# Two-layer graph network on one core: bias matmul, softmax division and loops of the stage between the layers, rewritten

## Chip, cores and metric

One NeuronCore of a Trainium2 chip. The metric is the device time of one execution in microseconds (us).

## What is computed

A graph of N = 6250 nodes with 128 features and E = 106250 edges sorted by destination. The reference, cut to what matters:

```python
h = relu(layernorm(x))
# layer 0: softmax over the edges of each node, feature by feature, then a linear layer
msg   = h[src] + edge_attr
e     = exp(msg*beta - segment_max(msg*beta)[dst])
denom = segment_sum(e, dst)                      # [N, 128]
agg   = segment_sum(msg * e / denom[dst], dst)   # [N, 128]
x     = x + (agg @ H + bias + h)                 # H: 128x128 from phm_rule and W
# layer 1: graph attention, 4 heads
h  = relu(layernorm(x))
Wx = h @ W.T                                     # [N, 128], then edge scores, softmax, sum, elu
x  = x + elu(attention(Wx, a, src, dst))
```

The bias is a row of 128 float32 numbers, drawn at random, so it is not zero.

## The kernel before

**Edges.** Edges go in 208 groups of 512. In both layers GpSimd issues indirect DMAs for the rows of the source nodes, TensorE turns tiles and sums edges into nodes by one-hot matmuls, VectorE scans for the running maximum, and ScalarE takes exponentials and adds each group's sums to `acc`, in which the nodes lie along the free axis: `acc[:, 0, n]` is the numerator of node n and `acc[:, 1, n]` its denominator, with the 128 features on the partitions. The last group of layer 0 is merged by `L659`.

**Between the layers.** 6250 nodes are 49 tiles of 128, in 13 batches (`NBAT`) of 4 tiles (`GE` = 512 nodes), of which the last has one tile of 106 nodes. For each batch:

- `invert0` (VectorE, `L958`): reciprocal of the 512 denominators of each partition into `inv`, one of two buffers that lie in `ring_h`.
- `average0` (GpSimd, `L577`): numerator times reciprocal into `aggT`, one of two buffers, also in `ring_h`. From the third batch on it waits for `mid_out` of two batches before.
- `layer_out` (TensorE): for each of the 4 tiles, a float32 matmul of `aggT` with the matrix `phm` (`L1156`), and a float32 matmul that adds the bias, with a row of ones as its weights, one partition deep (`L1158`). It writes one of two PSUM banks of `sums`.
- `finish0` (VectorE): adds the result to `nodes` (`L966`), and takes statistics of the 4 tiles for the layer norm (`statistics`, `L768`).

When all 13 batches are measured, `norm_all_nodes` makes the scale and shift of every node (22 small VectorE instructions, `L777` to `L790`). Then GpSimd copies those of a batch to `norm_b` (`numbers1`, `L530`), ScalarE makes relu of the normalised tiles (`h1`, `L699`), TensorE turns them (`L1169`) and multiplies by W (`L1181`), VectorE copies out, and SyncE stores the rows that layer 1 gathers.

**Order.** Each engine has a loop written by hand, `sweep(eng, count, unroll, stages)`: step s calls every stage for item s - lag, in the order listed. VectorE has `[(3, finish0), (0, invert0)]`, GpSimd `[(1, average0)]`, TensorE `[(2, layer_out)]`. The first and last steps are written out and those between are a hardware loop (`Fori`). Engines wait for one another by semaphores alone.

Of the kernel before, what the change touches and what calls it, by code (L numbers as in the profile page):

```python
# [56 lines left out]


def gnn_kernel(nc, x_in, src_in, dst_in, ea_in, rule_in, w0_in, bias_in, beta_in, w1_in, a_in, out):
    N, D = x_in.shape
# [13 lines left out]
    LAST = N - (NT - 1) * P  # L78
    NBAT = -(-NT // GB)
# [11 lines left out]
    HRING = 4  # L91
# [3 lines left out]
    with ctx:  # L95
        def sb(name, shape, dt=F32):
            return ctx.enter_context(nc.sbuf_tensor(name, shape, dt))

        def sem(name):
            return ctx.enter_context(nc.semaphore(name))  # L100

        def sems(name, n):
            return [sem(f"{name}{i}") for i in range(n)]
# [8 lines left out]
        ident = sb("ident", [P, P])  # L112
# [7 lines left out]
        ones_row = sb("ones_row", [1, P])  # L120
        junk = sb("junk", [1, 1])
        zero_row = sb("zero_row", [1, WIN], BF16)
        beta = sb("beta", [P, 1])
        bias_row = sb("bias_row", [1, D])
# [20 lines left out]
        nodes = sb("nodes", [P, NT, D])  # L145
        hn = sb("hn", [P, 2, GB, D])
# [10 lines left out]
        inv = ring_h[:, 0:2, :]  # L157
# [12 lines left out]
        acc = sb("acc", [P, 2, N + WIN])  # L170
# [13 lines left out]
        prod = sb("prod", [P, 2, GB, D])  # L184
        onehot = sb("onehot", [P, RING, GB, P])
        onehotT = sb("onehotT", [P, 2, GE])
        logit_v = sb("logit_v", [P, GB * H])
        logit = sb("logit", [P, WGT, GB * H])
        logit_d = sb("logit_d", [P, 2, GB * H])
# [5 lines left out]
        sums = ctx.enter_context(nc.psum_tensor("sums", [P, 2, 2, WIN], F32))  # L195
# [4 lines left out]
        bank = [ctx.enter_context(nc.psum_tensor(f"bank{i}", [P, GE], F32)) for i in range(4)]  # L200
# [31 lines left out]
        normed = sem("normed")  # L232
# [2 lines left out]
        ln0_part = sem("ln0_part")  # L235
        ln0_sum = sems("ln0_sum", WXB)
        h_stored = sems("h_stored", WXB)
        mid_inv = sem("mid_inv")
        mid_agg = sem("mid_agg")
        mid_out = sem("mid_out")  # L240
        mid_numbers = sem("mid_numbers")
        mid_h = sem("mid_h")
        mid_hT_psum = sem("mid_hT_psum")
        mid_hT = sem("mid_hT")
# [44 lines left out]
        L0, L1 = layer_sems(0), layer_sems(1)  # L289
# [20 lines left out]
        def _(sp):  # L310
# [176 lines left out]
        def _(pool):  # L487
# [32 lines left out]
            pool.memset(ones_row[:, :], 1.0).then_inc(self_pool, 1)  # L520
# [41 lines left out]

            sweep_edges(pool, [(0, gather0)])

            def numbers1(b, u, use):
                if later(b, 2):
                    pool.wait_ge(mid_h, b - 1)
                batch_numbers(b, u, mid_numbers)


            def average0(b, u, use):
                w = LAST if isinstance(b, int) and b == NBAT - 1 else GE
                pool.wait_ge(mid_inv, b + 1)
                if later(b, 2):
                    pool.wait_ge(mid_out, b - 1)
                apart(pool)
                pool.tensor_tensor(aggT[:, u, 0:w], acc[:, 0, bass.ds(b * GE, w)], inv[:, u, 0:w], ALU.mult  # L577
                                   ).then_inc(mid_agg, 1)
# [32 lines left out]
        def _(act):  # L611
# [78 lines left out]
            sweep_edges(act, [(5, merge0), (0, lift0), (3, weigh0)])  # L690


            def h1(b, u, use):
                act.wait_ge(mid_numbers, b + 1)
                if later(b, 2):
                    act.wait_ge(mid_hT_psum, b - 1)
                apart(act)
                for t in range(1 if isinstance(b, int) and b == NBAT - 1 else GB):
                    ins = act.activation(hn[:, u, t, :], nodes[:, bass.ds(b * GB + t, 1), :].rearrange("p a d -> p (a d)"),  # L699
                                         ACT.Relu, bias=norm_b[:, u, 1, t:t + 1], scale=norm_b[:, u, 0, t:t + 1])  # L700
                ins.then_inc(mid_h, 1)

            sweep(act, NBAT, 2, [(0, h1)])

            def weigh1(g, s, use):
                act.wait_ge(L1["shifted"], g + 1)
# [45 lines left out]
        def _(dve):  # L752
# [201 lines left out]
            def invert0(b, u, use):  # L954
                w = LAST if isinstance(b, int) and b == NBAT - 1 else GE
                if later(b, 2):
                    dve.wait_ge(mid_agg, b - 1)
                dve.reciprocal(inv[:, u, 0:w], acc[:, 1, bass.ds(b * GE, w)]).then_inc(mid_inv, 1)  # L958

            def finish0(b, u, use):  # L960
                last = isinstance(b, int) and b == NBAT - 1
# [3 lines left out]
                tiles = nodes[0:rows, b * GB:b * GB + 1, :] if last else nodes[:, bass.ds(b * GB, GB), :]  # L965
                dve.tensor_tensor(tiles, tiles, sums[0:rows, u, 0, 0:t * D].rearrange("p (t d) -> p t d", d=D), ALU.add  # L966
                                  ).then_inc(self_res, 1)
# [109 lines left out]
        def _(pe):  # L1077
# [68 lines left out]
            def layer_out(b, u, use):
                last = isinstance(b, int) and b == NBAT - 1
                pe.wait_ge(mid_agg, b + 1)
                if later(b, 2):
# [3 lines left out]
                for t in range(1 if last else GB):  # L1153
                    rows = LAST if last else P
                    where = sums[0:rows, u, 0, t * D:(t + 1) * D]
                    pe.matmul(where, aggT[:, u, t * P:t * P + rows], phm[:, :, :].rearrange("p j b -> p (j b)"),  # L1156
                              start=True, stop=False, skip_group_check=True)
                    ins = pe.matmul(where, ones_row[0:1, 0:rows], bias_row[0:1, :], start=False, stop=True,  # L1158
                                    skip_group_check=True)
                ins.then_inc(mid_out, 1)  # L1160

            sweep(pe, NBAT, 2, [(2, layer_out)])

            def turn_h(b, u, use):
                pe.wait_ge(mid_h, b + 1)
# [103 lines left out]
```

## Time and profile before

| | |
|---|---|
| time, median of 3 runs | 2384.46 us (2381.5 to 2385.74) |
| time of the profiled execution | 2380.09 us |
| its span | 2378.3 us |
| TensorE busy | 1833.2 us, 77% |
| VectorE busy | 2133.7 us, 90% |
| ScalarE busy | 1335.0 us, 56% |
| GpSimd busy | 1647.5 us, 69% |
| TensorE's mean granted clock, 1 is 2.4 GHz | 0.935 |

The profiled execution took 1.79 us more than its span, which goes from the first instruction to the last. Busy shares are means over four unlike stages: start, layer 0, the stage between the layers, and layer 1. Everything of the change lies in the third, which is some 3% of the span, so the rows below are those of that stage, with some from elsewhere that show what an instruction of a kind takes.

### The profile page before, as it was taken

Reading aid. Unit: us, or ns where it says so; the run is one execution under the profiler, and the core shown is the slowest. Engines: PE = TensorE matmul, PEld = TensorE weight load, DVE = VectorE, ACT = ScalarE, POOL = GpSimd, SP = SyncE. Lnnn points to the kernel's source line nnn. Section 1 sums busy time; section 2 is a strip of 40 time slices with the busy share of each in tenths; the row PEclk is TensorE's granted clock in tenths of the full one; section 3 lists DMA queues with packets and bytes.
Section 4 is the critical chain, followed back from the end, with each engine's and each line's share of the span. In section 5 each row is a group of like instructions: output and inputs, shape, how many; then the busy total and the mean of one; then the engine's idle time right before and its main releaser. Section 6 shows DMA issues by size and latency. Waiting matters only on the chain.

```text
span 2378.3 us, 61655 instructions
## 1 busy us (share of the span) xinstructions
PE 1833.2 (77%) x14239; PEld 1681.1 (71%) x14240; DVE 2133.7 (90%) x4065; ACT 1335.0 (56%) x3451; POOL 1647.5 (69%) x1748
## 2 busy tenths in 40 slices
PE   0466666666666766666787989999999998999986
PEld 0466666666666666666566888888888888888886
DVE  5799999999999999999766888888888888898885
ACT  2366666666666666666223555555555555555554
POOL 3677777777777777777115777777777777777761
PEclk9999999999999999999757999999999999999985
DMA  5544444444444444443003333333333333333321
GB/s 126 143 131 129 131 129 130 131 127 124 130 127 132 129 130 131 129 130 108 3 15 87 61 59 60 59 58 59 59 59 58 58 59 59 59 59 58 59 52 54
DMA packets 338740, 214.13 MB, mean 90 GB/s; under 512 B 170817, under 2 KB 305197, under 8 KB 338686
## 3 DMA queue, kind: packets, MB, share of 16 engines
q0 software_dynamic: 53248, 112.57, 20.0%
q1 hardware_dynamic: 285438, 100.94, 16.6%
q8 instruction: 22, 0.36, 0.1%
q14 instruction: 32, 0.26, 0.0%
HBM read 201.32 MB, written 10.30 MB: 89 GB/s over the span
## 4 chain that ended last, share of the span: by engine, by line
POOL 44%; issue 20%; DVE 18%; PE 6%; DMA 6%; SPq 3%; ACT 2%; DVEq 1%; POOLq 1%; ACTq 0%
POOL msg L590 24%; POOL ring_h L559 20%; DVE seg_max L900 5%; DVE run_max L897 3%; DMA ring_h<-h_dram,meta_g 3%; DMA msg<-wx_dram,meta_g 3%; DVE sums L897 2%; DVE prod L935 2%; DVE msg L918 2%; PE sums L1156 1%; PE sums L1158 1%; SPq L457 1%; PE sums L1115 1%; DVE onehot L944 1%; DVE onehot L881 1%
## 5 line engine op out<-in xcount | busy, mean ns | idle before, releaser
L559 POOL DMA_INDIRECT ring_h<-h_dram,meta_g x832 | 809.6, 973 | 259.9 <-issue 258.4
L590 POOL DMA_INDIRECT msg<-wx_dram,meta_g x832 | 792.6, 953 | 264.6 <-issue 246.0
L1115 PE MATMUL sums<-onehot,prod 128*128 128x128 f32 x3328 | 697.3, 293 | 25.0 <-ACT acc L659 12.8
L1115 PE MATMUL sums<-onehot,wgt 128*128 128x128 f32 x3328 | 678.5, 288 | 0.0
L1115 PEld LDWEIGHTS sums<-onehot,prod 128*128 128x128 f32 x3328 | 538.5, 204 | 71.0 <-issue 68.1
L1115 PEld LDWEIGHTS sums<-onehot,wgt 128*128 128x128 f32 x3328 | 540.2, 204 | 0.0
L1124 PE MATMUL bank<-beta_ident,msg 128*128 128x128 f32 x1664 | 245.7, 292 | 341.9 <-DVE msg L918 341.8
L1124 PEld LDWEIGHTS bank<-beta_ident,msg 128*128 128x128 f32 x1664 | 205.5, 195 | 382.5 <-DVE msg L918 331.2
L659 ACT ACTIVATE acc<-sums 128x1022 f32 x414 | 423.7, 1023 | 0.0
L688 ACT ACTIVATE sums<-ring_h 128x512 f32<-128x512 f32 x208 | 125.1, 602 | 382.1 <-DMA ring_h<-h_dram,meta_g 381.9
L897 DVE TENSOR_TENSOR_SCAN sums<-flags,seg_max,bank 4x512 f32<-4x512 bf16 x207 | 264.0, 1275 | 5.8 <-PE bank L1211 4.4
L897 DVE TENSOR_TENSOR_SCAN run_max<-flags,run_max,bank 128x512 f32<-128x512 bf16 x207 | 263.5, 1273 | 0.0
L900 DVE TENSOR_TENSOR_SCAN seg_max<-flags,run_max 128x512 f32<-128x512 bf16 x208 | 254.6, 1224 | 7.1
L900 DVE TENSOR_TENSOR_SCAN seg_max<-flags,sums 4x512 f32<-4x512 bf16 x208 | 251.1, 1207 | 7.2
L651 ACT ACTIVATE carried<-acc,scale 128x2 f32 x414 | 120.9, 292 | 184.5 <-PE sums L1115 175.7
L1202 PEld LDWEIGHTS bank<-window,onehotT 128*128 128x128 f32 x1664 | 212.1, 200 | 4.1 <-ACT onehotT L721 2.9
L1202 PE MATMUL bank<-window,onehotT 128*128 128x4 f32 x1664 | 206.0, 247 | 2.8 <-DMA window<-wx_dram 1.3
L709 ACT ACTIVATE sums<-logit_d 128x16 f32<-128x16 f32 x208 | 39.0, 188 | 267.8 <-DVE logit_d L1022 266.0
L881 DVE TENSOR_SCALAR onehot<-iota_f,meta_g 128x128 f32<-128x128 f32 x832 | 180.4, 275 | 6.0 <-DMA meta_g<-meta 5.9
L918 DVE TENSOR_TENSOR msg<-msg,sums 128x512 f32<-128x512 f32 x208 | 141.0, 678 | 13.2 <-ACT sums L688 13.1
L1030 DVE TENSOR_TENSOR prod<-sums,msg 128x512 f32<-128x512 f32 x208 | 140.0, 673 | 4.8 <-PE sums L1115 4.5
L935 DVE TENSOR_TENSOR prod<-sums,msg 128x512 f32<-128x512 f32 x208 | 142.0, 683 | 1.8 <-ACT sums L676 1.8
(144 smaller groups left out, 2750.5 us busy)
## 6 DMA issues: line engine op xcount, KB each, us to landing
msg<-in_edge_attr SPq DMA_DIRECT2D x207, 256.0 KB, 3.1
flags<-flag_dram SPq DMA_DIRECT2D x52, 512.2 KB
ring_h<-h_dram,meta_g POOLq DMA_INDIRECT x832
msg<-wx_dram,meta_g POOLq DMA_INDIRECT x832
window<-wx_dram SPq DMA_DIRECT2D x832, 2.0 KB
wx_dram<-msg SPq DMA_DIRECT2D x13, 272.0 KB, 2.5
nodes<-in_x SPq DMA_DIRECT2D x4, 768.0 KB, 8.3
h_dram<-wgt SPq DMA_DIRECT2D x12, 256.0 KB, 2.4
```

Source lines behind the costliest of these rows:

```text
L559: pool.indirect_dma_start(hg[:, s % HRING, b, :], None, h_dram, bass.IndirectOffsetOnAxis(ap=meta_g[:, s, b:b + 1], axis=0)).then_inc(L0[" ...
L590: pool.indirect_dma_start(msg[:, s, b, :], None, wx_dram, bass.IndirectOffsetOnAxis(ap=meta_g[:, s, b:b + 1], axis=0)).then_inc(L1["gather ...
L659: act.activation(acc[:, :, bass.ds(node + 1, WIN - 1)], sums[:, par, :, 1:WIN], ACT.Copy).then_inc(k["merged"], 1)
L881: ins = dve.tensor_scalar(onehot[:, s, b, :], iota_f[:, :], key[:, b:b + 1], None, ALU.is_equal)
L897: dve.tensor_tensor_scan(run, flag[:, 0:GE], data, before, ALU.add, ALU.max).then_inc(k["scanned"], 1)
L900: dve.tensor_tensor_scan(seg_max[0:n, par, ::-1], flag[:, GE:0:-1], run[:, ::-1], -BIG, ALU.add, ALU.max).then_inc(k["scanned"], 1)
L918: dve.tensor_tensor(msg[:, s, :, 0:D], msg[:, s, :, 0:D], row_psum.rearrange("p (b d) -> p b d", b=GB), ALU.add).then_inc(L0["added"], 1)
L935: dve.tensor_tensor(prod[:, s % 2, :, :], wgt_psum.rearrange("p (b d) -> p b d", b=GB), msg[:, s, :, 0:D], ALU.mult).then_inc(L0["multipli ...
L1030: dve.tensor_tensor(prod[:, s % 2, :, :].rearrange("p b (h d) -> p b h d", h=H), head, msg[:, s, :, 0:D].rearrange("p b (h d) -> p b h d", ...
L1115: ins = pe.matmul(sums[:, 0, j, bass.ds(off, P)], what[:, slot, b, :], onehot[:, s, b, :], start=(b == 0), stop=(b == GB - 1), skip_group_ ...
L1124: ins = pe.matmul(bank[s % 2][:, b * P:(b + 1) * P], msg[:, s, b, 0:D], beta_ident[:, :], start=True, stop=True)
L1202: ins = pe.matmul(bank[2][:, b * H:(b + 1) * H], onehotT[:, s % 2, b * P:(b + 1) * P], window[:, s, b, :], start=True, stop=True)
```

## The change

**Bias.** The bias row is loaded onto all 128 partitions (`bias_all`), and VectorE splits it into three bfloat16 parts, high, middle and low, whose sum is the float32 number. A tile `bias_parts` has the three parts in its first three partitions and zero in the others, repeated for the 4 tiles of a batch. One bfloat16 matmul of all 128 partitions against ones (`ones_parts`), 512 columns wide, puts the bias under a batch before the four `phm` matmuls add to it. The splitting is nine VectorE instructions after the layer 0 loop and ahead of its wait for the last merge.

**Division.** ScalarE takes `Ln` of the denominators and then `Exp` with scale -1 twice, once into a PSUM bank and once into `ring_h`: both are a first guess r of 1/d (`seed0`). GpSimd multiplies d by r (`polish0`). VectorE makes (d r - 2) r in PSUM and then multiplies that by -1 and by the numerator (`divide0`), which is one Newton step and the division. `ring_h` and the banks are rings of four, `diff` of two.

**Loops.** `sweep` gives way to `straight`, which writes all 13 batches out. VectorE's order is now `divide0` of batch s, then `finish0` of batch s - 2. `h1` reads the scale and shift from `norm` itself, so GpSimd's copies to `norm_b` for layer 1 go.

```diff
+def straight(count, stages):
+    for s in range(count + max(lag for lag, _ in stages)):
+        for lag, stage in stages:
+            if 0 <= s - lag < count:
+                stage(s - lag)
...
-            sp.dma_start(bias_row[:, :], bias_in.rearrange("(a d) -> a d", a=1)).then_inc(weights_in, 16)
+            sp.dma_start(bias_all[:, :], bias_in.rearrange("(a d) -> a d", a=1).to_broadcast([P, D])).then_inc(weights_in, 16)
...
-            sweep(pool, NBAT, 2, [(1, average0)])
-            pool.wait_ge(normed, 2)
-            sweep(pool, NBAT, 2, [(0, numbers1)])
+            def polish0(b):
+                w = LAST if b == NBAT - 1 else GE
+                pool.wait_ge(mid_seed, b + 1)
+                if b >= 2:
+                    pool.wait_ge(mid_inv, b - 1)
+                pool.tensor_tensor(diff[:, b % 2, 0:w], acc[:, 1, b * GE:b * GE + w], ring_h[:, b % HRING, 0:w], ALU.mult
+                                   ).then_inc(mid_near, 1)
+            straight(NBAT, [(0, polish0)])
...
+            act.wait_ge(L0["merged"], NG)
+            def seed0(b):
+                w = LAST if b == NBAT - 1 else GE
+                if b >= HRING:
+                    act.wait_ge(mid_out, b - HRING + 1)
+                near = ring_h[:, b % HRING, 0:w]
+                act.activation(near, acc[:, 1, b * GE:b * GE + w], ACT.Ln).then_inc(mid_log, 1)
+                act.wait_ge(mid_log, b + 1)
+                act.activation(bank[b % HRING][:, 0:w], near, ACT.Exp, scale=-1.0)
+                act.activation(near, near, ACT.Exp, scale=-1.0).then_inc(mid_seed, 1)
+            straight(NBAT, [(0, seed0)])
+            act.wait_ge(normed, 2)
...
+            part_of_bias(dve.tensor_copy(bias_hi, bias_all[:, :]))
+            part_of_bias(dve.tensor_tensor(bias_rest, bias_all[:, :], bias_hi, ALU.subtract))
...
-                dve.reciprocal(inv[:, u, 0:w], acc[:, 1, bass.ds(b * GE, w)]).then_inc(mid_inv, 1)
+            def divide0(b):
+                w = LAST if b == NBAT - 1 else GE
+                near = bank[b % HRING][:, 0:w]
+                dve.wait_ge(mid_near, b + 1)
+                dve.scalar_tensor_tensor(near, diff[:, b % 2, 0:w], 2.0, near, ALU.subtract, ALU.mult).then_inc(mid_inv, 1)
+                dve.wait_ge(mid_inv, b + 1)
+                dve.scalar_tensor_tensor(ring_h[:, b % HRING, 0:w], near, -1.0, acc[:, 0, b * GE:b * GE + w],
+                                         ALU.mult, ALU.mult).then_inc(mid_agg, 1)
...
-            sweep(dve, NBAT, 2, [(3, finish0), (0, invert0)])
+            straight(NBAT, [(0, divide0), (2, finish0)])
...
+            def layer_out(b):
+                last = b == NBAT - 1
+                t, rows = (1, LAST) if last else (GB, P)
+                if b >= 2:
+                    pe.wait_ge(self_res, b - 1)
+                elif b == 0:
+                    pe.wait_ge(L0["merged"], NG)
+                pe.matmul(sums[0:rows, b % 2, 0, 0:t * D], ones_parts[:, 0:rows],
+                          bias_parts[:, 0:t, :].rearrange("p t d -> p (t d)"), start=True, stop=False, skip_group_check=True)
+                pe.wait_ge(mid_agg, b + 1)
+                for i in range(t):
+                    ins = pe.matmul(sums[0:rows, b % 2, 0, i * D:(i + 1) * D],
+                                    ring_h[:, b % HRING, i * P:i * P + rows], phm[:, :, :].rearrange("p j b -> p (j b)"),
+                                    start=False, stop=(i == t - 1), skip_group_check=True)
+                ins.then_inc(mid_out, 1)
+            straight(NBAT, [(0, layer_out)])
```

## Rows read from the trace of the kernel before

**Rows 1.** Stretches of the middle stage, and one in layer 1 (windows: busy us and count).
```profile
core 0: us, PE busy (x) PEld busy (x) DVE busy (x) ACT busy (x) POOL busy (x), PEclk, DMA share, GB/s
...
1153.05:1157.90 4.85, 0.00 (x0) 0.00 (x0) 4.85 (x2) 0.00 (x0) 1.28 (x1) 0.76 0.00 0
1157.90:1229.70 71.80, 70.85 (x196) 48.80 (x196) 55.05 (x74) 0.00 (x0) 14.48 (x12) 0.50 0.00 0
1229.70:1235.27 5.57, 0.00 (x0) 0.00 (x0) 4.42 (x22) 0.00 (x0) 0.28 (x2) 0.50 0.00 0
...
1288.00:1295.40 7.40, 6.90 (x35) 6.54 (x36) 6.93 (x18) 1.98 (x5) 5.57 (x7) 0.50 0.34 62
```

**Rows 2.** Groups by line and shape, 1140 to 1260 us (busy us, mean ns, idle before).
```profile
L1156 PE MATMUL sums<-phm,ring_h 128*128 128x128 f32 x96 | 38.2, 501 | 6.8 <-POOL ring_h L577 6.8
L1158 PE MATMUL sums<-bias_row,ones_row 1*128 1x128 f32 x96 | 38.1, 498 | 0.0
...
L958 DVE RECIPROCAL ring_h<-acc 128x512 f32<-128x512 f32 x6 | 19.8, 3324 | 6.4 <-ACT acc L659 6.4
L699 ACT ACTIVATE hn<-nodes,norm_b 128x128 f32 x40 | 15.7, 480 | 0.3 <-PE bank L1169 0.3
L577 POOL TENSOR_TENSOR ring_h<-acc,ring_h 128x512 f32<-128x512 f32 x12 | 15.4, 1280 | 71.3 <-PE sums L1158 43.4 <-DVE ring_h L958 27.9
```

**Rows 3.** Waits, 1153 to 1229.7 us (total us, times, longest).
```profile
POOL ring_h L577 <- PE sums L1158: 47.9, 11, 4.6
```

**Rows 4.** Timeline of VectorE in the middle stage (start us, us).
```profile
1181.31 0.69 DVE L966 TENSOR_TENSOR nodes<-nodes,sums 128x512 f32 x1 [1.01 <-PE sums L1158]
...
1187.08 0.69 DVE L966 TENSOR_TENSOR nodes<-nodes,sums 128x512 f32 x1 [0.56 <-PE sums L1158]
...
1215.88 0.69 DVE L966 TENSOR_TENSOR nodes<-nodes,sums 128x512 f32<-128x512 f32 x1 [0.52 <-PE sums L1158]
1216.67 0.87 DVE L768 BATCH_NORM_STATS2 stats<-nodes 128x6 f32<-128x128 f32 x4
1217.46 0.80 DVE L958 RECIPROCAL ring_h<-acc 128x106 f32<-128x106 f32 x1
```

**Rows 5.** Timeline of ScalarE near the end of the kernel.
```profile
2340.97 0.63 ACT L735 ACTIVATE elu_e<-ring_h 128x512 f32<-128x512 f32 x1 [2.98 <-DVE ring_h L1049]
2341.63 0.63 ACT L737 ACTIVATE elu_e<-elu_e 128x512 f32<-128x512 f32 x1
2342.17 0.61 ACT L745 ACTIVATE hn<-acc 128x512 f32<-128x512 f32 x1
```

**Rows 6.** Timeline of GpSimd and TensorE in the stage.
```profile
1156.56 1.28 POOL L577 TENSOR_TENSOR ring_h<-acc,ring_h 128x512 f32<-128x512 f32 x1 [25.95 <-DVE ring_h L958]
...
1157.94 0.76 PE L1156 MATMUL sums<-phm,ring_h 128*128 128x128 f32 x2 [6.82 <-POOL ring_h L577]
...
1187.13 1.28 POOL L577 TENSOR_TENSOR ring_h<-acc,ring_h 128x512 f32<-128x512 f32 x1 [4.50 <-PE sums L1158]
```

**Rows 7.** Timeline of VectorE in layer 0, two independent instructions.
```profile
1083.51 0.68 DVE L918 TENSOR_TENSOR msg<-msg,sums 128x512 f32<-128x512 f32 x1
...
1084.11 0.69 DVE L944 TENSOR_TENSOR onehot<-bank,meta_g 128x512 f32<-128x512 f32 x1
```

**Rows 8.** Timeline of TensorE in layer 1, inside the last stretch of rows 1.
```profile
1292.57 0.63 PE L1115 MATMUL sums<-onehot,prod 128*128 128x128 f32 x2
1292.99 0.63 PE L1115 MATMUL sums<-onehot,wgt 128*128 128x128 f32 x2
```

**Rows 9.** Timeline of ScalarE at its first instructions.
```profile
30.80 1.28 ACT L630 ACT_TABLE_LOAD   x1 [30.67 <-PE bank L1086]
...
32.09 0.28 ACT L630 ACTIVATE meta<-bank 128x128 int32<-128x128 f32 x1
```

**Rows 10.** Groups by line and shape, whole span, VectorE: two SCALAR_TENSOR_TENSOR groups.
```profile
L1063 DVE SCALAR_TENSOR_TENSOR pos<-ring_h,nodes 128x512 f32<-128x512 f32 x12 | 8.2, 682 | 0.2 <-DVE ring_h L1049 0.2
...
L845 DVE SCALAR_TENSOR_TENSOR nodes<-run_max,nodes 128x512 f32 x4 | 3.8, 954 | 0.0
```

More of the change, by code:

```diff
@@ L119, in gnn_kernel @@
         head_pick = sb("head_pick", [P, H])
-        ones_row = sb("ones_row", [1, P])
         junk = sb("junk", [1, 1])
@@ L123, in gnn_kernel @@
         beta = sb("beta", [P, 1])
-        bias_row = sb("bias_row", [1, D])
+        bias_all = sb("bias_all", [P, D])
+        bias_parts = sb("bias_parts", [P, GB, D], BF16)
+        ones_parts = sb("ones_parts", [P, P], BF16)
         rule_rep = sb("rule_rep", [P, PH, PH])
@@ L156, in gnn_kernel @@
         hg = ring_h[:, :, :].rearrange("p r (b d) -> p r b d", d=D)
-        inv = ring_h[:, 0:2, :]
         inv_head = sb("inv_head", [P, GB * H])
@@ L186, in gnn_kernel @@
         onehotT = sb("onehotT", [P, 2, GE])
+        bias_hi, bias_mid, bias_lo = (hn[:, 0, i, :].bitcast(BF16)[:, 0:D] for i in range(3))
+        bias_rest = hn[:, 1, 0, :]
         logit_v = sb("logit_v", [P, GB * H])
@@ L237, in gnn_kernel @@
         h_stored = sems("h_stored", WXB)
+        bias_step = sem("bias_step")
+        bias_made = sem("bias_made")
+        mid_log = sem("mid_log")
+        mid_seed = sem("mid_seed")
+        mid_near = sem("mid_near")
         mid_inv = sem("mid_inv")
@@ L240, in gnn_kernel @@
         mid_out = sem("mid_out")
-        mid_numbers = sem("mid_numbers")
         mid_h = sem("mid_h")
@@ L519, in _ @@
             pool.tensor_copy(iota_f[:, :], iota_i[:, :]).then_inc(self_pool, 1)
-            pool.memset(ones_row[:, :], 1.0).then_inc(self_pool, 1)
+            pool.memset(ones_parts[:, :], 1.0).then_inc(self_pool, 1)
             pool.memset(zero_row[:, :], 0.0).then_inc(self_pool, 1)
@@ L563, in _ @@
             sweep_edges(pool, [(0, gather0)])
[L565 to L578, printed above, removed]
-            sweep(pool, NBAT, 2, [(1, average0)])
-            pool.wait_ge(normed, 2)
-            sweep(pool, NBAT, 2, [(0, numbers1)])
+            def polish0(b):
[6 more added lines that the diff above has]
+            straight(NBAT, [(0, polish0)])
             def gather1(g, s, use):
@@ L690, in _, with h1 @@
             sweep_edges(act, [(5, merge0), (0, lift0), (3, weigh0)])
-            def h1(b, u, use):
-                act.wait_ge(mid_numbers, b + 1)
-                if later(b, 2):
+            act.wait_ge(L0["merged"], NG)
[10 more added lines that the diff above has]
+            act.wait_ge(normed, 2)
+            def h1(b):
+                if b >= 2:
                     act.wait_ge(mid_hT_psum, b - 1)
[L697 to L700, printed above, removed]
+                for t in range(1 if b == NBAT - 1 else GB):
+                    n = b * GB + t
+                    ins = act.activation(hn[:, b % 2, t, :], nodes[:, n, :], ACT.Relu,
+                                         bias=norm[:, 1, n:n + 1], scale=norm[:, 0, n:n + 1])
                 ins.then_inc(mid_h, 1)
-            sweep(act, NBAT, 2, [(0, h1)])
+            straight(NBAT, [(0, h1)])
             def weigh1(g, s, use):
@@ L949, in _, with part_of_bias, finish0 @@
             sweep_edges(dve, [(0, add0), (0, one_hot0), (3, products0), (1, maxima0)])
-            dve.wait_ge(L0["merged"], NG)
[L954 to L957, printed above, removed]
-                dve.reciprocal(inv[:, u, 0:w], acc[:, 1, bass.ds(b * GE, w)]).then_inc(mid_inv, 1)
-            def finish0(b, u, use):
-                last = isinstance(b, int) and b == NBAT - 1
+            parts = [0]
+            def part_of_bias(ins):
+                parts[0] += 1
+                ins.then_inc(bias_step, 1)
+                dve.wait_ge(bias_step, parts[0])
+            part_of_bias(dve.tensor_copy(bias_hi, bias_all[:, :]))
+            part_of_bias(dve.tensor_tensor(bias_rest, bias_all[:, :], bias_hi, ALU.subtract))
+            part_of_bias(dve.tensor_copy(bias_mid, bias_rest))
+            part_of_bias(dve.tensor_tensor(bias_rest, bias_rest, bias_mid, ALU.subtract))
+            part_of_bias(dve.tensor_copy(bias_lo, bias_rest))
+            part_of_bias(dve.tensor_scalar(bias_rest, bias_hi, ident[:, 0:1], None, ALU.mult))
+            part_of_bias(dve.scalar_tensor_tensor(bias_rest, bias_mid, ident[:, 1:2], bias_rest, ALU.mult, ALU.add))
+            part_of_bias(dve.scalar_tensor_tensor(bias_rest, bias_lo, ident[:, 2:3], bias_rest, ALU.mult, ALU.add))
+            dve.tensor_copy(bias_parts[:, :, :], bias_rest.rearrange("p (a d) -> p a d", a=1).to_broadcast([P, GB, D])
+                            ).then_inc(bias_made, 1)
+            dve.wait_ge(L0["merged"], NG)
+            def divide0(b):
[6 more added lines that the diff above has]
+                                         ALU.mult, ALU.mult).then_inc(mid_agg, 1)
+            def finish0(b):
+                last = b == NBAT - 1
                 t = 1 if last else GB
@@ L964, in finish0 @@
                 dve.wait_ge(mid_out, b + 1)
-                tiles = nodes[0:rows, b * GB:b * GB + 1, :] if last else nodes[:, bass.ds(b * GB, GB), :]
-                dve.tensor_tensor(tiles, tiles, sums[0:rows, u, 0, 0:t * D].rearrange("p (t d) -> p t d", d=D), ALU.add
+                tiles = nodes[0:rows, b * GB:b * GB + t, :]
+                dve.tensor_tensor(tiles, tiles, sums[0:rows, b % 2, 0, 0:t * D].rearrange("p (t d) -> p t d", d=D), ALU.add
                                   ).then_inc(self_res, 1)
@@ L1144, in _ @@
             pe.wait_ge(phm_ready, 1)
[L1146 to L1149, printed above, removed]
+            pe.wait_ge(bias_made, 1)
+            def layer_out(b):
+                last = b == NBAT - 1
+                t, rows = (1, LAST) if last else (GB, P)
+                if b >= 2:
                     pe.wait_ge(self_res, b - 1)
@@ L1152, in layer_out @@
                     pe.wait_ge(L0["merged"], NG)
[L1153 to L1159, printed above, removed]
+                pe.matmul(sums[0:rows, b % 2, 0, 0:t * D], ones_parts[:, 0:rows],
[5 more added lines that the diff above has]
+                                    start=False, stop=(i == t - 1), skip_group_check=True)
                 ins.then_inc(mid_out, 1)
-            sweep(pe, NBAT, 2, [(2, layer_out)])
+            straight(NBAT, [(0, layer_out)])
             def turn_h(b, u, use):
```

## The prediction

> **What bounds the stage now.** I cut the span into stretches [rows 1], then took the groups [rows 2], the waits [rows 3] and the timeline [rows 4] of the middle one. The stage starts at 1153.05, when ScalarE's last merge lets the first reciprocal go, and ends at 1229.70 with the last statistics: 76.65 us. For 71.80 of these TensorE is busy 70.85, so it sets the pace; VectorE is busy 55.05, ScalarE not at all, GpSimd 14.48 [rows 1]. The waits agree: GpSimd waits 47.9 us for the bias matmul L1158 [rows 3], and VectorE's adds wait for it too [rows 4]. One batch takes 1187.08 - 1181.31 = 5.77 us [rows 4]. A float32 matmul shows as two records, so a batch is 16 passes, half of them bias, and the two groups have equal busy time, 38.2 and 38.1 us [rows 2].
>
> Two things make those passes dear. TensorE's granted clock is 0.50 (1.2 GHz) for the whole stretch although it is never idle; it fell in the 6.82 us pause before the first matmul [rows 1, 6]. And a pair of passes takes, by the batch, 5.77/8 = 0.72 us, that is 0.36 a pass [rows 4], while in layer 1, at the same clock, two passes of the same shape take 1292.99 - 1292.57 = 0.42 us, 0.21 a pass [rows 1, 8]. The difference is that L1156 (128 partitions) and L1158 (1 partition) take turns.
>
> **TensorE after.** Per batch: one bf16 matmul of 512 columns and 8 float32 passes, all 128 partitions deep. The passes by rows 8: 8 x 0.21 = 1.7 us. The bf16 matmul has no row; from below it is one pass, 0.21, from above four, 0.85. I take the middle, 0.4: 2.1 us a batch at 1.2 GHz, less if the clock rises. The bf16 one stands ahead of the wait for `mid_agg`, so it fills a pause. TensorE falls from 5.77 to 2.1 us a batch and no longer sets the pace.
>
> **VectorE after.** The reciprocal, 3.32 us [rows 2], goes. Two scalar_tensor_tensor of 512 columns come, each with one operand in PSUM. Nearest rows: 0.68 for that operation from SBUF [rows 10], 0.68 to 0.69 for a tensor_tensor with one operand in PSUM [rows 4, 7]. Independent neighbours start 1084.11 - 1083.51 = 0.60 apart [rows 7]. The second needs the first's result, for which I take its 0.69 and 0.03 more: 0.72. The add to its statistics is 1216.67 - 1215.88 = 0.79, the statistics to the next instruction 1217.46 - 1216.67 = 0.79 [rows 4]. A batch: 0.72 + 0.60 + 0.79 + 0.79 = 2.90 us, of which the division is 1.32 and the finish 1.58. Bounds: four times 0.60 for the wide and 0.79 below, 2.6; above, each wide instruction 0.95 as in L845 [rows 10], 3.7.
>
> **ScalarE and GpSimd after.** ScalarE was idle. An instruction of 512 columns takes 0.63; one that needs the last starts 0.66 after it, one that doesn't 0.54 [rows 5]. A batch: 0.66 + 0.54 + 0.54 = 1.74 us. GpSimd keeps one tensor_tensor of 1.28 us [rows 2]. Both are under 2.90 and hidden. The rings don't bind: ScalarE waits for the matmuls of four batches before, GpSimd for the division of two before. `Ln` is new: the trace has one table load, 1.28 us, with the first instruction 0.01 us behind it [rows 9], and none later for Exp. I charge one on the path, between the merge and the first Ln (bounds 0 and 2 x 1.28).
>
> **Fill.** From 1153.05: load 1.28; first seed 0.66 + 0.54 + 0.63 = 1.83; hop to GpSimd 0.15 (the first reciprocal, 3.32, ends near 1156.4 and GpSimd starts at 1156.56 [rows 2, 6]); 1.28; hop 0.10 (1157.84 to 1157.94 [rows 6]). The first division starts at 4.64 us, the third, paced by ScalarE, at 4.64 + 2 x 1.74 = 8.12. From there VectorE has work without a gap: its first finish is due at 9.4, when TensorE, which had the first quotient at 4.64 + 1.41 = 6.05, needs 2.1.
>
> **Sum.** From 8.12: 10 divisions x 1.32 = 13.2, 12 finishes x 1.58 = 19.0, the short last batch some 1.2 (an estimate, a quarter of the columns with the fixed part): 33.4. The stage takes 8.1 + 33.4 = 41.5 us instead of 76.65: 35.1 less.
>
> **Other edits.** Between the last normalisation and `h1` GpSimd's copies go: the stretch of 5.57 us has 4.42 of VectorE and 0.28 of GpSimd [rows 1], so 0.3 less. `h1` itself is bound by ScalarE (15.7 us for 40 with 0.3 idle [rows 2]) and stays. The nine bias instructions: even at 0.69 each, 6.2 us, they fit into VectorE's 6.4 us of waiting for the last merge [rows 2] plus 4.64 until its first division; without that cover they would cost up to 6.2. The wider bias load and the memset lie in the start-up, 0. The straight loops drop the branches; VectorE's pieces of 2.90 are from parts already written out, so nothing more is booked. Layer 1 is only moved earlier. Total 35.4 us.
>
> The profiled execution took 2380.09, so its like would take 2344.7; against the median of the runs, 2384.46, which is 4.4 higher, 2349. I give that.
>
> **One table or two.** The rows show one load for Exp and the rest, and cannot show where Ln belongs [rows 9]. The Trainium skill (ScalarE: Activation LUTs, "Table sets: the hidden batching unit") names a set that holds exp and ln together, so that ln followed by exp costs one load. By it the sum is the one above; without it the next paragraph but one holds. No run so far shows it.
>
> **Rivals.**
>
> *TensorE still sets the pace.* If the 0.36 a pass is a property of L1156 and not of the turns with L1158, a batch is 8 x 0.36 + 0.4 = 3.3 us. From the first quotient at 6.15, 12 x 3.3 + 0.9 + 0.7: the stage takes 47.4, 29 less, total 2355. For it: 0.36 is what both lines show. Against: L1115's 0.42 a pair [rows 8]. The Trainium skill (TensorEngine Tiling, "Key Properties") says that changing the tiling mode drains TensorE; a matmul one partition deep between full ones could be such a change, which the change ends. That would fit 0.36 against 0.21 but isn't shown by them.
>
> *Tables change with each function.* If Ln and Exp each call for a load, ScalarE's batch is 0.66 + 0.54 + 0.63 + 2 x 1.28 = 4.4 us and it sets the pace: 12 x 4.4, the short batch 3.3, and 2.6 to the end: 58.7, 18 less, 2366. Every us on a load's price adds 26 us; from 2.0 us a load on the change loses. The row gives 1.28, on an idle engine. The same page of the Trainium skill ("What ACT_TABLE_LOAD costs") puts 2.66 us on a switch with its drain; by that this case would come out some 18 us slower.
>
> *VectorE and GpSimd hinder each other.* L845 took 0.95 beside GpSimd's work where L1063 took 0.68 [rows 10]. If each batch loses GpSimd's 1.28, 15 us come back: 20 less, 2364. Against: L966 at 1187.08 is 0.69 although GpSimd's 1.28 from 1187.13 runs beside it [rows 4, 6]; all wide instructions after have an operand in PSUM.
>
> *The batches don't overlap* (the other side). If seed, polish, division, matmuls and finish run one after another, a batch is 1.83 + 0.15 + 1.28 + 0.10 + 1.41 + 0.10 + 1.9 + 1.66 = 8.4 us, 104 in all, 27 slower, 2411. It loses from 6.2 us a batch on. Against: no wait in the code ties batch b + 1 to b.
>
> **Chances.** Forecast 0.68, TensorE's pace 0.07, VectorE with GpSimd 0.07, tables at 1.28 each 0.11, tables at 2 us or more 0.03, no overlap 0.02, no change to tell 0.02. Without a load on the path and with the 4.4 us of the profiled execution the forecast reaches down to 2343; VectorE's upper bound of 3.7 us adds 10, to 2359. The range 2342 to 2368 takes in all but the slow cases. A difference under 0.2%, 5 us, can't be told from none: faster 0.93, same 0.02, slower 0.05.
>
> **What would show it.** TensorE's passes near 0.21 us at a clock of 0.50 (or 0.11 at 1), busy under 30 us in the stage; VectorE without idle time after the first three divisions and 2.90 us a batch; no or one table load after layer 0; the last statistics some 41 us after the last merge; layer 1 as long as before. I am wrong if ScalarE is the one without idle time, if GpSimd's 1.28 or VectorE's 0.69 stretch, or if layer 1 takes a different time.

## The result, and the profile after

The changed kernel takes 2368.35 us (median of 5 runs, 2366.12 to 2407.49) against 2385.74 us (median of 5, 2381.5 to 2425.98) for the kernel before beside it. The ratio is 0.9937, with an interval of 0.9925 to 0.9949: faster by 0.6%, some 15 us, where the forecast was 35. Some executions, the kernel before's too, come out about 40 us longer, nearly all of it in layer 0 (42 of 45 us in the run before_again below); the ratios leave them out.

The profiled execution took 2366.12 us, 13.97 less than the 2380.09 of before. First the stretches: the last merge with the first seed, the stage itself, the normalisation.

```profile
core 0: us, PE busy (x) PEld busy (x) DVE busy (x) ACT busy (x) POOL busy (x), PEclk, DMA share, GB/s
1154.70:1160.41 5.71, 0.59 (x1) 0.10 (x1) 0.00 (x0) 5.63 (x7) 1.09 (x1) 0.50 0.01 3
1160.41:1215.93 55.52, 28.34 (x110) 23.48 (x110) 35.16 (x88) 49.84 (x59) 12.38 (x12) 0.50 0.00 0
1215.93:1221.10 5.17, 0.00 (x0) 0.00 (x0) 4.41 (x21) 0.00 (x1) 0.00 (x0) 0.50 0.00 0
```

From last merge to last statistics it is 61.2 us instead of 76.65 [rows 1]. TensorE, busy for 70.85 us there before, is busy for under 29; VectorE, the next in the forecast, for 35. The one that is nearly always busy is ScalarE, which before did nothing: 5.63 + 49.84 = 55.5 us. The groups of the stage by line and shape say with what (busy us, mean ns, idle before):

```profile
L1200 PE MATMUL sums<-phm,ring_h 128*128 128x128 f32 x96 | 23.3, 424 | 8.3 <-DVE ring_h L998 8.3
L705 ACT ACT_TABLE_LOAD x13 | 16.7, 1283 | 0.2
L707 ACT ACT_TABLE_LOAD x13 | 16.7, 1283 | 0.2
...
L584 POOL TENSOR_TENSOR diff<-acc,ring_h 128x512 f32<-128x512 f32 x12 | 13.1, 1091 | 64.4 <-ACT ring_h L708 64.4
L996 DVE SCALAR_TENSOR_TENSOR bank<-diff,bank 128x512 f32<-128x512 f32 x12 | 8.4, 696 | 28.7 <-POOL diff L584 28.7
L998 DVE SCALAR_TENSOR_TENSOR ring_h<-bank,acc 128x512 f32<-128x512 f32 x12 | 8.3, 691 | 0.4
```

There are 26 table loads, one ahead of every `Ln` (L705) and one ahead of the first `Exp` of every batch (L707): 26 x 1.283 = 33.4 of ScalarE's 55.5 us. The forecast had one. The longest waits of the stage (us in total, times, longest) follow from it and run down the chain: GpSimd for ScalarE's seed, VectorE for GpSimd's product, TensorE for VectorE's add. Of GpSimd's 66.7 us, 28.0 are the first wait, which began in layer 0. Before, GpSimd waited most for the bias matmul [rows 3].

```profile
POOL diff L584 <- ACT ring_h L708: 66.7, 13, 28.0
DVE bank L996 <- POOL diff L584: 28.7, 12, 10.2
...
PE sums L1196 <- DVE nodes L1007: 21.7, 10, 2.9
```

One batch in the timeline (start us, us), to set beside the 5.77 us between two L966 before [rows 4]:

```profile
1172.33 1.28 ACT L705 ACT_TABLE_LOAD   x1
1172.39 1.09 POOL L584 TENSOR_TENSOR diff<-acc,ring_h 128x512 f32<-128x512 f32 x1 [3.31 <-ACT ring_h L708]
1173.52 0.70 DVE L996 SCALAR_TENSOR_TENSOR bank<-diff,bank 128x512 f32<-128x512 f32 x1 [1.41 <-POOL diff L584]
1173.63 0.63 ACT L705 ACTIVATE ring_h<-acc 128x512 f32<-128x512 f32 x1
...
1174.27 1.28 ACT L707 ACT_TABLE_LOAD   x1
...
1175.57 0.60 ACT L707 ACTIVATE bank<-ring_h 128x512 f32<-128x512 f32 x1
1175.59 0.61 PE L1196 MATMUL sums<-bias_parts,ones_parts 128*128 128x512 bf16 x1 [2.09 <-DVE nodes L1007]
...
1175.99 1.92 PE L1200 MATMUL sums<-phm,ring_h 128*128 128x128 f32 x8
1176.11 0.61 ACT L708 ACTIVATE ring_h<-ring_h 128x512 f32<-128x512 f32 x1
1176.74 1.28 ACT L705 ACT_TABLE_LOAD   x1
```

Load, Ln, load, Exp, Exp, and the next load: 1176.74 - 1172.33 = 4.41 us a batch, with no gap on ScalarE above 0.02 us. Every other engine shows a wait in it, GpSimd 3.31, VectorE 1.41, TensorE 2.09.

The 13.97 us by milestones, before and after (from the timelines; "norm" is VectorE's last instruction of the normalisation, the end that of the profiled execution's time):

| stretch | before | after | difference |
|---|---|---|---|
| start to layer 0's last merge | 1153.02 | 1154.70 | +1.7 |
| last merge to last statistics | 76.68 | 61.22 | -15.5 |
| statistics to norm | 5.14 | 5.14 | 0.0 |
| norm to first gather of layer 1 | 29.62 | 30.47 | +0.85 |
| first gather to layer 1's last merge | 1072.29 | 1072.01 | -0.3 |
| last merge to the end of the run | 43.34 | 42.58 | -0.8 |

### The profile page after: what moved, and what is told of

It reads as the page before. It is cut to its first block, busy times and chain, and to the rows that moved or that the text cites. A ratio compares the mean times of both kernels' runs of the same rounds, so it can differ in the third digit from the quotient of the medians.

```text
span 2364.4 us, 61321 instructions
## 1 busy us (share of the span) xinstructions
PE 1784.6 (75%) x14154; PEld 1649.2 (70%) x14155; DVE 2110.9 (89%) x4087; ACT 1390.4 (59%) x3516; POOL 1641.5 (69%) x1735
## 4 chain that ended last, share of the span: by engine, by line
POOL 56%; issue 24%; DMA 7%; DVE 6%; PE 2%; ACT 2%; SPq 1%; POOLq 1%; DVEq 0%; ACTq 0%
POOL ring_h L573 28%; POOL msg L595 28%; DMA ring_h<-h_dram,meta_g 4%; DMA msg<-wx_dram,meta_g 2%; DVE sums L917 1%; DVE seg_max L920 1%; PE sums L1156 1%; DVE onehot L901 1%; DVE prod L1071 1%; POOL diff L584 1%; ACT sums L693 1%; ACT acc L664 0%; PE bank L1281 0%; PE bank L1224 0%; SPq L331 0%
## 5 line engine op out<-in xcount | busy, mean ns | idle before, releaser
L1156 PE MATMUL sums<-onehot,prod 128*128 128x128 f32 x3328 | 696.2, 293 | 28.7 <-ACT acc L664 14.6
```

What stands on the lines that cost most here:

```text
L1156: ins = pe.matmul(sums[:, 0, j, bass.ds(off, P)], what[:, slot, b, :], onehot[:, s, b, :], start=(b == 0), stop=(b == GB - 1), skip_group_ ...
```

## The experiments

Two theories stood after the result. Loads: ScalarE's 26 table loads set the pace, and with one load the stage is the one forecast. The other: the loads sit where VectorE, TensorE or the hops between engines would take the time anyway.

**one_load.** The set of tables that serves Ln and Exp together is loaded explicitly, ahead of ScalarE's first activation; nothing else differs from the changed kernel.

```
+            act.add_instruction(mybir.InstLoadActFuncSet(..., act_func_set_id=6, ins=[], outs=[]))
             act.wait_ge(const_ready, 1)
```

> The changed kernel with one edit: ahead of its first activation ScalarE loads the table set that holds Ln and Exp together, so the whole kernel has 1 table load instead of 27. Theory A (the 26 loads of the middle stage, 33.4 us of ScalarE, set its pace of 4.40 us a batch): VectorE sets the pace with 2.90 us, the stage goes from 61.2 to about 40.2 us and the kernel from 2368 to about 2347. Theory B (the loads lie beside something else that takes 4.4 us a batch, such as the chain from seed to finish or GpSimd beside VectorE): the stage stays at 55 us or more and the time above 2362.

Measured: 2347.21 us, ratio to before 0.985 [0.9833, 0.9866]. The trace has one table load in all. The stage as one window:

```profile
1154.13:1193.78 39.65, 21.97 (x109) 19.31 (x111) 34.26 (x88) 21.58 (x39) 13.48 (x13) 0.71 0.00 1
```

VectorE's timeline:

```profile
1166.38 0.68 DVE L998 SCALAR_TENSOR_TENSOR bank<-diff,bank 128x512 f32<-128x512 f32 x1
1167.09 0.69 DVE L1000 SCALAR_TENSOR_TENSOR ring_h<-bank,acc 128x512 f32<-128x512 f32 x1
1167.70 0.68 DVE L1009 TENSOR_TENSOR nodes<-nodes,sums 128x512 f32<-128x512 f32 x1
1168.48 0.87 DVE L790 BATCH_NORM_STATS2 stats<-nodes 128x6 f32<-128x128 f32 x4
1169.27 0.68 DVE L998 SCALAR_TENSOR_TENSOR bank<-diff,bank 128x512 f32<-128x512 f32 x1
```

Without the loads VectorE has no idle time and a batch is 1169.27 - 1166.38 = 2.89 us. The stage is 21.6 us shorter than in the changed kernel. The other theory falls: nothing but the loads was taken away, and these 21.6 us went with them.

**ln_pairs.** The loads stay, but two batches share them: Ln, Ln, then the four Exps.

```
+            def guess0(b):
...
-            straight(NBAT, [(0, seed0)])
+            for first in range(0, NBAT, 2):
+                for stage in (seed0, guess0):
+                    for b in range(first, min(first + 2, NBAT)):
+                        stage(b)
```

> The changed kernel with the Ln of two batches ahead of the Exp of the two, so 14 loads in the stage instead of 26, with the separate table sets as they are. Theory A: ScalarE needs 0.54 + 0.65 + 1.28 + 3 x 0.54 + 0.63 + 1.28 = 6.0 us for two batches, 3.0 each, just over VectorE's 2.90; stage about 43 us, kernel about 2350. Theory B: stage stays at 55 us or more, above 2362.

Measured: 2351.59 us, ratio 0.9873 [0.9857, 0.989]. The stage as one window:

```profile
1154.70:1200.72 46.02, 24.23 (x109) 20.75 (x111) 34.57 (x88) 38.77 (x53) 13.23 (x13) 0.63 0.00 1
```

ScalarE's timeline:

```profile
1173.90 1.15 ACT L705 ACTIVATE ring_h<-acc 128x512 f32<-128x512 f32 x2
1175.07 1.28 ACT L711 ACT_TABLE_LOAD   x1
...
1178.57 1.28 ACT L705 ACT_TABLE_LOAD   x1
1179.86 1.15 ACT L705 ACTIVATE ring_h<-acc 128x512 f32<-128x512 f32 x2
```

With 14 loads a pair of batches takes 1179.86 - 1173.90 = 5.96 us, as expected. The stage is 46.0, not the 43 expected: the first division waits for both Lns, and VectorE waited again (3.10 us at 1166.79) before the pairs came evenly. 12 loads fewer are worth 15.2 us of the stage, 1.27 each, close to the 1.28 that a load lasts; but part of that is luck. In the even stretch a pair of batches is 2 x 4.41 - 5.96 = 2.86 us shorter, 2.57 of it two loads and 0.3 activations that start closer together, and some 2 us of the gain are lost again at the two ends.

**division_alone.** The changed kernel with the bias added as before, four float32 matmuls of one partition a batch.

```
-                pe.matmul(sums[...], ones_parts[:, 0:rows], bias_parts[...], start=True, stop=False, ...)
...
+                    pe.matmul(where, ring_h[...], phm[...], start=True, stop=False, skip_group_check=True)
+                    ins = pe.matmul(where, ones_row[0:1, 0:rows], bias_all[0:1, :], start=False, stop=True, ...)
```

> The change without its bias part: division, loops and h1 as changed, but each phm matmul followed again by the float32 bias matmul one partition deep. If TensorE's 16 passes at 0.36 us, 5.77 us a batch, are the bound that the bias part removes, the stage takes fill 6 + 12 x 5.77 + 2.5 = 78 us, no better than the 76.65 of the kernel before, kernel 2381 to 2387. If the division was the bound before, it gives most of the 15 us: about 2370.

Measured: 2384.52 us, ratio 1.0011 [1.0, 1.0022]. The stage as one window, and TensorE's timeline:

```profile
1155.54:1234.60 79.06, 70.86 (x196) 48.75 (x196) 35.50 (x88) 55.48 (x66) 13.47 (x13) 0.51 0.00 1
```
```profile
1180.16 0.80 PE L1181 MATMUL sums<-phm,ring_h 128*128 128x128 f32 x2
1180.88 0.79 PE L1183 MATMUL sums<-bias_all,ones_row 1*128 1x128 f32 x2
1181.61 0.80 PE L1181 MATMUL sums<-phm,ring_h 128*128 128x128 f32 x2
```

TensorE is busy 70.86 us, as long as before, and a pair of records starts every 0.72 us. The new division, with its loads, gives nothing while the old bias stays.

**bias_alone.** The other half: the kernel before with only the bias part (three bf16 rows, one matmul of 512 columns); VectorE keeps the reciprocal, GpSimd the product.

```
-                    ins = pe.matmul(where, ones_row[0:1, 0:rows], bias_row[0:1, :], start=False, stop=True, ...)
...
+                pe.matmul(sums[...], ones_parts[:, 0:rows], bias_parts[...], start=True, stop=False, ...)
```

> The kernel before with the bias part alone: reciprocal, GpSimd product and hardware loops as before. TensorE falls to 2.1 us a batch; VectorE sets the pace with reciprocal 3.3, add and statistics 1.85: 5.1 us a batch, stage about 62 us instead of 76.65, kernel about 2370 (14 less). That would be all that the whole change gives, and the division with its table loads gives nothing. If the 0.36 us a pass does not come from the bias matmul, TensorE keeps 3.3 us a batch and the result is the same for the time, but the passes show it.

Measured: 2366.57 us, ratio 0.9926 [0.9906, 0.9946], the same as the whole change within both intervals. The stage as one window, and VectorE's timeline:

```profile
1155.00:1215.37 60.37, 27.96 (x110) 23.77 (x111) 58.28 (x75) 0.00 (x0) 15.71 (x13) 0.52 0.00 0
```
```profile
1166.24 3.33 DVE L981 RECIPROCAL ring_h<-acc 128x512 f32<-128x512 f32 x1
1169.49 0.63 DVE L989 TENSOR_TENSOR nodes<-nodes,sums 128x512 f32<-128x512 f32 x1
1170.22 0.87 DVE L773 BATCH_NORM_STATS2 stats<-nodes 128x6 f32<-128x128 f32 x4
1171.01 3.34 DVE L981 RECIPROCAL ring_h<-acc 128x512 f32<-128x512 f32 x1
```

VectorE has no idle time and 4.77 us a batch, 3.25 of them the reciprocal. So the stage takes 60.4 us with the old division and 61.2 with the new one: the 26 loads take all that the removed reciprocal gives.

The next kernels ask why the old bias was dear, and what the stage takes without the loads. They ran on another chip, where at that time every run, the kernel before's too, took 3292 to 3390 us: layer 0 moved 92 GB/s there, where the profile after shows 122 to 144. The middle stage moves next to nothing, and three kernels run on both chips had stages of 61.83 and 61.81, 34.00 and 34.06, 24.58 and 25.03 us. So the stage is read there and the ratio from the other chip.

**bias_deep_f32.** The kernel before, with the same 16 float32 passes a batch; only the bias matmuls are 128 partitions deep (row 0 holds the bias, the others zeros).

```
+            link(dve.tensor_scalar(bias_deep[:, :], bias_row[:, :], ident[:, 0:1], None, ALU.mult))
...
-                    ins = pe.matmul(where, ones_row[0:1, 0:rows], bias_row[0:1, :], start=False, stop=True,
+                    ins = pe.matmul(where, ones_row[:, 0:rows], bias_deep[:, :], start=False, stop=True,
...
```

> The kernel before with one edit: the float32 bias matmul is 128 partitions deep (ones in all of them as weights, the bias in the first and zeros in the others) instead of one. The count of passes stays 16 a batch. Theory C (the turns between a one-deep and a full matmul make a pass 0.36 us): passes fall to 0.21 us at a clock of 0.50, TensorE needs 3.4 us a batch, VectorE sets the pace with its 4.8 to 5.1 us, the stage takes about 61 us and the kernel about 2368, as with the bias part. Theory D (accumulating twice into the same PSUM columns, or something in the phm matmul, makes it): passes stay at 0.36 us, stage 77 us, kernel 2384.

Measured: 3341.64 us against 3365.67, ratio 0.9945 [0.9906, 0.9984]. The stage as one window:

```profile
1567.98:1629.81 61.83, 34.14 (x196) 31.57 (x196) 58.38 (x75) 0.00 (x1) 15.69 (x13) 0.75 0.00 0
```

The same number of records (196) takes TensorE 34.14 us instead of 70.85 [rows 1], and the granted clock is 0.75 over the stretch instead of 0.50. VectorE sets the pace with 58.38, as in bias_alone.

**one_load_deep.** one_load with the four deep float32 bias matmuls: 16 passes a batch under the faster VectorE.

```
+                    pe.matmul(where, ring_h[...], phm[...], start=True, stop=False, skip_group_check=True)
+                    ins = pe.matmul(where, ones_deep[:, 0:rows], bias_deep[:, :], start=False, stop=True, ...)
```

> The kernel with one table load, its bf16 bias matmul replaced by four float32 ones, 128 partitions deep: 16 passes a batch. Theory C with the clock staying at 0.50: 16 x 0.21 = 3.4 us a batch on TensorE, over VectorE's 2.90, stage about 48 us, kernel about 2355. If the clock rises to 1 under the full-depth passes: 1.8 us, VectorE keeps the pace, 2347 as with one load. Theory D: 5.8 us a batch, 2385.

Measured: 3331.85 us, ratio 0.9907 [0.9871, 0.9942]. The stage as one window, and TensorE's timeline:

```profile
1564.36:1604.57 40.21, 26.29 (x196) 24.21 (x196) 34.36 (x88) 21.75 (x39) 13.49 (x13) 0.92 0.00 1
```
```profile
1571.35 0.63 PE L1187 MATMUL sums<-bias_deep,ones_deep 128*128 128x128 f32 x2
1571.77 0.63 PE L1185 MATMUL sums<-phm,ring_h 128*128 128x128 f32 x2
1572.20 0.45 PE L1187 MATMUL sums<-bias_deep,ones_deep 128*128 128x128 f32 x2
1572.48 0.39 PE L1185 MATMUL sums<-phm,ring_h 128*128 128x128 f32 x2
1572.71 0.39 PE L1187 MATMUL sums<-bias_deep,ones_deep 128*128 128x128 f32 x2
```

The timeline shows both rates: a pair every 0.42 us until 1572.20, every 0.22 to 0.23 from 1572.48 on. Between them the granted clock goes from 0.50 to 1 (2.4 GHz), in windows of 1 us with the columns of the first table of stretches:

```profile
1571.00:1572.00 1.00, 1.00 (x7) 1.00 (x7) 0.97 (x2) 0.30 (x1) 0.62 (x1) 0.50 0.00 0
1572.00:1573.00 1.00, 1.00 (x9) 1.00 (x9) 0.54 (x2) 0.32 (x1) 0.47 (x1) 0.84 0.00 0
1573.00:1574.00 1.00, 1.00 (x11) 1.00 (x11) 0.90 (x4) 0.97 (x3) 0.00 (x0) 1.00 0.00 0
```

The stage is within 0.6 us of one_load's. So the number of passes was not the trouble in the kernel before. Taking turns with matmuls one partition deep a pass costs 0.36 us, at full depth 0.21 at the same clock: 16 x 0.21 = 3.4 us a batch, under VectorE's 4.77 there. Under the new division's 2.89 even 3.4 would have been the bound; here the clock rose, as it did in the stage of no run with the one-deep matmuls.

**no_newton.** one_load without the Newton step: GpSimd multiplies the sum by the Exp's guess.

```
-                pool.tensor_tensor(diff[:, b % 2, 0:w], acc[:, 1, ...], ring_h[...], ALU.mult).then_inc(mid_near, 1)
+                pool.tensor_tensor(ring_h[...], acc[:, 0, ...], ring_h[...], ALU.mult).then_inc(mid_agg, 1)
...
-            straight(NBAT, [(0, divide0), (2, finish0)])
+            straight(NBAT, [(0, finish0)])
```

> The kernel with one table load, and the Newton step left out: GpSimd multiplies the numerator by the Exp guess itself, so the division is only as exact as Ln and Exp. VectorE keeps add and statistics, 1.6 us a batch; GpSimd 1.3, ScalarE 1.2. TensorE becomes the bound with 2.1 to 2.3 us at a clock of 0.50: stage about 31 us, kernel about 2339. If the clock rises to 1, VectorE's 1.6 us: stage 24, kernel 2332. If VectorE was not the bound at 2.90, nothing changes: 2347.

Measured: 3307.0 us, ratio 0.9856 [0.9792, 0.9921], stage 24.58 us. Of the expected branches it is the one with VectorE at 1.6 us a batch: the granted clock was 0.87 over the stage, and TensorE didn't set the pace.

**shared.** one_load with the last product of the division on GpSimd; the sign goes into the weights, once.

```
+            def average0(b):
...
+                pool.tensor_tensor(ring_h[...], acc[:, 0, ...], run_max[:, b % 2, 0:w], ALU.mult).then_inc(mid_agg, 1)
+            straight(NBAT, [(0, polish0), (1, average0)])
...
+                dve.scalar_tensor_tensor(run_max[...], diff[...], 2.0, bank[...][...], ALU.subtract, ALU.mult)
```

> The kernel with one table load, and the last product of the division moved from VectorE to GpSimd: VectorE writes (d r - 2) r to SBUF, GpSimd multiplies it by the numerator, and phm is negated once at the start. Work as in the change. VectorE 0.60 + 0.79 + 0.79 = 2.2 us a batch, GpSimd 1.09 + 1.28 = 2.4 with its hops 2.5: GpSimd or TensorE (2.1 to 2.3) sets the pace. Stage about 36 us, kernel about 2342, 5 under one load. If GpSimd's waits for its own results cost more than 0.5 us a batch, no gain over one load: 2347 or above.

Measured: 3325.12 us, ratio 0.9882 [0.9824, 0.994], stage 34.00 us, where 36 were expected: GpSimd's two products follow each other without a gap, so a batch is 2.3 us and not 2.5.

**shared_again, no_newton_again, deep_f32_again.** The three kernels unchanged, on the chip of the first four, for ratios that can be set beside those.

> The kernel of the run shared, again, on another chip if one comes up: its stage took 34.0 us there, 6 less than with one load, but layers 0 and 1 were both far longer on that chip. With layers as on the first chip: 2347 - 6 = about 2341. If the rest of the kernel eats the gain: 2347.

> The kernel of the run no_newton again (one table load, the Newton step left out): stage 24.6 us there, 15 less than with one load. With layers as on the first chip: 2347 - 15 = about 2332.

> The kernel of the run bias_deep_f32 again (the kernel before with the float32 bias matmul 128 partitions deep): stage 61.8 us there, 15 less than before. With layers as on the first chip about 2369.

Measured: shared_again 2339.36 us, 0.9823 [0.9809, 0.9837]; no_newton_again 2331.54 us, 0.9791 [0.9777, 0.9805]; deep_f32_again 0.9938 [0.9919, 0.9957] (2366.14 to 2370.17 us in the three runs behind the ratio), where the whole change has 0.9937. The stage of shared_again as one window, its GpSimd groups by shape, and the stage of no_newton_again as one window:

```profile
1154.39:1188.45 34.06, 20.29 (x109) 15.81 (x111) 26.16 (x75) 21.70 (x40) 28.35 (x26) 0.80 0.00 1
```
```profile
L590 POOL TENSOR_TENSOR ring_h<-acc,run_max 128x512 f32<-128x512 f32 x12 | 15.4, 1286 | 0.0
L584 POOL TENSOR_TENSOR diff<-acc,ring_h 128x512 f32<-128x512 f32 x12 | 13.1, 1090 | 25.3 <-ACT ring_h L716 25.3
```
```profile
1155.71:1180.74 25.03, 17.42 (x109) 15.47 (x111) 18.30 (x62) 15.11 (x27) 15.50 (x13) 0.86 0.00 1
```

In shared_again GpSimd is the busiest, and nearly all of its idle time is one wait for the first seed: the bound has moved from VectorE to it. shared_again is the fastest kernel that does all of the work, 1.8% under before, where the change has 0.6%. The Newton step (with the second Exp that feeds it) costs the difference of the stages, 34.06 - 25.03 = 9.0 us, in that form and 39.65 - 25.03 = 14.6 in one_load's.

**before_again.** The kernel before once more, to see whether layer 0's 1.7 us are the change's.

> The kernel before, unchanged, profiled once more. Its layer 0 ended at 1153.02 us; in the changed kernel and the four experiments on the first chip it ended at 1154.1 to 1155.5. If this is scatter between executions it ends anywhere in 1153 to 1156 here; if the change costs layer 0 a microsecond or two, it ends near 1153.0 again. The middle stage takes 76.6 to 76.7 us as before.

Inconclusive: its one execution took 2424.82 us, and its layer 0 was 42 us longer than before's, so it can't tell 1.7. Its stage, 76.7 us, is that of before. It ran on the chip of the long runs, where layer 0 now moved 118 to 140 GB/s: what made every kernel 40% longer there had passed.

## Why the prediction was wrong

The step that failed is one sentence: "I charge one on the path, between the merge and the first Ln (bounds 0 and 2 x 1.28)". There were 26, 33.4 us of ScalarE, and they made it the bound. The bounds allowed for two loads' worth of time at most. The price of one was right, 1.28 us; the count was wrong. [rows 9] showed one load for all functions used so far, which says nothing of a function not yet used. The text said so and still gave the case with a load at each change 0.14.

The stages show the order of the bounds, per batch:

| kernel | bound | us a batch | stage, us |
|---|---|---|---|
| before | TensorE | 5.77 | 76.7 |
| division_alone | TensorE | 5.8 | 79.1 |
| bias_alone | VectorE, reciprocal | 4.77 | 60.4 |
| the change | ScalarE, loads | 4.41 | 61.2 |
| ln_pairs | ScalarE, half the loads | 2.98 | 46.0 |
| one_load | VectorE | 2.89 | 39.7 |
| shared_again | GpSimd | 2.3 | 34.1 |
| no_newton_again | VectorE | 1.57 | 25.0 |

(5.8 is eight starts of 0.72, 2.3 the distance of two of GpSimd's products L584, 1.57 that of two adds.)

Point by point:

- **TensorE was the bound, because of the turns.** Shown: the rival "TensorE still sets the pace" falls with the changed kernel itself, where the eight passes L1200 follow the bf16 matmul by 0.40 us and take 1.92. bias_deep_f32 and one_load_deep show that depth alone makes the difference; whether the array drains between the two forms, no trace shows. The 0.4 us taken for the bf16 matmul was 0.40, and TensorE's batch 2.1 us, as forecast (from 1210.81 to 1212.92, one batch's bias matmul to the next).
- **VectorE 2.90 us a batch.** Right, 2.89, but hidden under ScalarE's 4.41 until the loads were gone. Its lower bound of 2.6 has a slip: it comes from three wide instructions at 0.60, not four.
- **GpSimd 1.28.** 1.09 in the new product; not on the path. Why it is less than 1.28 is open: it no longer writes over its operand, but neither does L590 in shared_again, and that takes 1.29. The rival of VectorE and GpSimd in each other's way: in one_load VectorE's wide instructions stay at 0.67 to 0.70 beside GpSimd's. That rival falls.
- **Sum.** 41.5 us with one load, so 40.2 without; one_load has 39.65. The pieces fit too: there the third division starts 6.45 us after the merge (6.84 by the forecast without the load), and from it to the end it is 33.2 (33.4). The forecast was right for a kernel that it was not given. That the profiled execution, 2345.57 us, lies so near the 2344.7 forecast is in part luck: the stage alone gave 37.0 us, and 2.5 came back elsewhere, 1.1 of them in layer 0.
- **The rival of the tables** had the batch, 4.4 us, and the total, 2366, almost right. Its stage of 58.7 was 2.5 short. From the last seed's end, 1210.93, to the last statistics it is 5.0 us and not 2.6, because VectorE does the finishes of three batches after it. Layer 0 and the other stretches make up the rest.
- **The price of a load.** The trace has 1283 ns, with 0.4 us of idle time ahead of all 26. The Trainium skill (ScalarE: Activation LUTs, "What ACT_TABLE_LOAD costs") gives the same 1283 ns but 2.66 us with the drain of a switch. No such drain is on the path here: the activation starts 0.01 to 0.02 us behind each load. The measurement decides. An estimate by the page's price, 26 x 1.38 = 36 us more, would have made the change slower than the kernel before.
- **One set for Ln and Exp.** The same page ("Table sets: the hidden batching unit") is right that such a set exists; one_load shows it. The kernel as built doesn't stay in it: where nobody asked for that set, each change of function came with a load.
- **The other edits.** The bias preparation ran from 1147.30 to 1150.25, inside VectorE's wait for the last merge, as said. The copies' 0.3 us: ScalarE's first `h1` instruction stands 0.04 us behind the norm, not 0.43. But from the norm to layer 1's first gather it was 0.85 us longer all the same; why, no run shows. Layer 1 took the same time.
- **What was missed besides.** The forecast booked the two halves as one sum. Taken apart, the bias half gives 0.7%, all that the change gives, and the division half gives nothing in division_alone, where the dear bias and the loads are left, and nothing in the change, where the loads are. No run has the dear bias without the loads; TensorE's 5.77 us a batch would bound it.
- **Open:** layer 0 ended 1.7 us later. All changed kernels on that chip end it 1.1 to 2.7 us later than before's one profiled execution (1154.13 to 1155.71), among them bias_alone, which adds next to nothing ahead of it. Scatter or the wider bias load: not settled. Runs of one kernel differ by more than that: the eight of the kernel before that stand behind shared_again's ratio go from 2379.69 to 2386.83.

## What to carry to other kernels

When a change brings a function that ScalarE has not used in this kernel, the trace of before cannot tell where its table lives: price one load at every change of function first, count the loads in the new trace first of all, and if they alternate, load a set that holds all of them once by hand. Where the second-busiest engine is close behind the first, each half of a change has to be priced under the bound that the other half leaves. A tiny matmul between full ones isn't cheap: put it in the form of its neighbours, or fold it into one of full depth.

## What the runs showed of the hardware

- A float32 matmul one partition deep between full ones costs 0.36 us a record, its neighbours too. At full depth, with the same columns and the same granted clock of 0.50 (1.2 GHz), it is 0.21. Zeros in 127 rows make it cheaper.
- The granted clock stayed at 0.50 for 72 us in before, with TensorE busy for 70.85 of them [rows 1], and at 0.51 over the stage in division_alone. With 16 full-depth passes a batch it went to 1 some 8 us after the last merge. In the changed kernel, where TensorE waits 2.09 us in every batch, it stayed at 0.50; in one_load it was 0.71 over the stage.
- 26 table loads took 1283 ns each, with no gap above 0.02 us in the batch shown, and the activations around them kept their 0.60 to 0.63 us.
- One chip ran every kernel, the one before too, 40% longer for a time, all of it outside the middle stage, which took the same time to within 0.5 us. Later the kernel before took 2424.82 us on it.
- A product of 128x512 float32 on GpSimd takes 1.09 us where the denominators are multiplied into `diff`, and 1.28 to 1.29 where the numerators are multiplied into `ring_h`, whether `ring_h` is also an operand (before, no_newton_again) or not (shared_again).
